# Hop fetches of edges without a successor: a bounds check and a cleared landing buffer, or a row of zeros in the table

## The reference

```python
A = 0.9 * segment_softmax(scores, head_ids)            # (edges, 4)
Z = broadcast(Z0[:, None, :], (nodes, 4, 64))
for _ in range(5):
    Z = segment_sum(A[:, :, None] * Z[tail_ids], head_ids) + 0.1 * Z0[:, None, :]
out = Z.reshape(nodes, 4 * 64) @ W_o
```

## Time and profile before

| | us |
|---|---|
| median of 3 runs | 11939.54 |
| lowest, highest | 11934.17, 11954.9 |
| span of the profiled execution, first to last instruction | 11926.9 |
| median over that span | 12.6 |
| window 2378 to 2916, hop 1 | 538 |
| window 4010 to 5046, hop 4 | 1036 |

### The profile page before, as it was taken

One profiled execution on the slowest core, in us unless ns is written; L12 is line 12 of the kernel. 1 busy time (PEld: TensorE's weight loads), 2 busy tenths in 40 slices (PEclk: granted clock), 3 DMA queues, 4 the chain that ended last, 5 costly groups with the idle time before them and its releaser, 6 DMA issues. The chain is left out here.

```text
span 11926.9 us, 102357 instructions
## 1 busy us (share of the span) xinstructions
PE 5189.3 (44%) x22423; PEld 3589.6 (30%) x22423; DVE 6264.4 (53%) x12751; ACT 2458.7 (21%) x4317; POOL 7982.4 (67%) x7869
## 2 busy tenths in 40 slices
PE   1719994000000244445655778833335422222245
PEld 1403221000000244444444556622224322222234
DVE  8931114887878544465555669933336533321127
ACT  0102221022222211122322333310003211000035
POOL 0767776776767677754766766567767677777730
PEclk9959997555555555576776777755555555555578
DMA  2412222554545211176654656622229833311148
GB/s 107 163 22 57 57 57 55 192 161 149 164 150 165 89 41 41 38 249 198 166 158 155 197 177 194 191 67 57 57 59 323 236 65 65 63 48 46 45 157 248
DMA packets 1247797, 1471.21 MB, mean 123 GB/s; under 512 B 843713, under 2 KB 948738, under 8 KB 1244410
## 3 DMA queue, kind: packets, MB, share of 16 engines
q1 hardware_dynamic: 951992, 1127.40, 29.9%
q0 software_dynamic: 277328, 269.94, 10.7%
q10 hardware_dynamic: 18290, 72.03, 1.5%
HBM read 830.95 MB, written 772.36 MB: 134 GB/s over the span
## 5 line engine op out<-in xcount | busy, mean ns | idle before, releaser
L2550 POOL DMA_INDIRECT r_got<-state,comb_src x1176 | 1209.8, 1029 | 454.9 <-issue 350.4
L330 POOL DMA_INDIRECT payload_or_bias_rows<-payload,place x784 | 885.2, 1129 | 587.4 <-POOLq L522 259.7
L1339 POOL DMA_INDIRECT hop_got<-edges_b,next_col x784 | 788.7, 1006 | 272.0 <-issue 238.5
L1339 POOL DMA_INDIRECT hop_got<-edges_a,next_col x784 | 782.1, 998 | 269.1 <-issue 238.4
L1588 PE MATMUL hop_ps_into<-hop_out,span_s 128*128 128x256 f32 (+1 forms) x10 | 5.6, 662 | 1966.6 <-DVE hop_out L1480 1965.8
L1528 ACT COPY hop_got<-hop_zeros 128x1792 f32<-128x1792 f32 x224 | 377.4, 1685 | 1508.7 <-DVE hop_ps_msg L1431 1099.0
L1588 PEld LDWEIGHTS hop_ps_into<-hop_out,span_s 128*128 128x128 f32 x10 | 2.5, 311 | 1969.1 <-DVE hop_out L1480 1968.1
L1480 DVE SCALAR_TENSOR_TENSOR hop_out<-hop_out,hop_runs_now,hop_ps_msg 128x256 f32<-128x256 f32 x1176 | 565.4, 481 | 51.0
L1351 POOL DMA_INDIRECT sum<-hop_out,put_s x392 | 432.3, 1103 | 119.5 <-issue 119.5
L2687 DVE TENSOR_REDUCE r_stat<-r_sq 128x14 f32<-128x896 f32 x196 | 211.9, 1081 | 567.8 <-ACT r_sq L2857 567.4
L2558 POOL DMA_INDIRECT x<-r_yt,put_t x392 | 403.8, 1030 | 146.6 <-issue 118.8
(11 more groups left out here) (727 smaller groups left out, 16895.6 us busy)
## 6 DMA issues: line engine op xcount, KB each, us to landing
edges_a<-hop_out SPq DMA_DIRECT2D x112, 896.0 KB
edges_b<-hop_out SPq DMA_DIRECT2D x112, 896.0 KB
hop_side<-x_dst SPq DMA_DIRECT2D x280, 224.0 KB, 4.0
r_in<-state SPq DMA_DIRECT2D x112, 448.0 KB, 4.9
x_and_sums<-c_y SPq DMA_DIRECT2D x56, 896.0 KB, 6.1
bn_in<-x_and_sums SPq DMA_DIRECT2D x56, 896.0 KB, 4.8
r_own<-state SPq DMA_DIRECT2D x84, 448.0 KB, 5.3
g_rows<-r_gx SPq DMA_DIRECT2D x84, 448.0 KB, 3.0
```

The costliest lines, as they stand in the source:

```text
L330: nc.gpsimd.indirect_dma_start(out=rows[:, n, :], out_offset=None, in_=t.pay, in_offset=bass.IndirectOffsetOnAxis(t.place[:, k, n:n + 1], ...
L1339: pool.indirect_dma_start(out=got[:, u, c, :], out_offset=None, in_=table, in_offset=at, bounds_check=EP - 1, oob_is_err=False).then_inc(g ...
L2550: pool.indirect_dma_start(out=got[:, n, c - b * CT, :], out_offset=None, in_=table, in_offset=bass.IndirectOffsetOnAxis(idx[:, at + c:at + ...
```

## The change

Hops no longer check the index, and the landing buffer is no longer cleared. An edge without a successor reads row EP of the table. The fetches of a chunk wait, in place of ACT's copy, for DVE's add of the chunk that used the same place before, four chunks earlier; `wait` issues nothing where the value is 0 or less, so the first four chunks wait for nothing. The semaphores `zeroed`, the tile `zeros`, DVE's fill and all of ACT's clearing copies go. Nothing else changes.

```diff
-        if heads and table is not None:
-            zeros = sb("zeros", [P, CT, G])
...
-        runs_ready, side_scaled, zeroed = sems("runs_ready"), sems("side_scaled"), sems("zeroed")
+        runs_ready, side_scaled = sems("runs_ready"), sems("side_scaled")
...
                 if heads:
-                    pool.wait_ge(zeroed[u], i + 1)
+                    wait(pool, added, n + 1 - RING)
...
                 for c in range(CT):
                     at = bass.IndirectOffsetOnAxis(idx[:, n * CT + c:n * CT + c + 1], 0)
-                    if heads:
-
-                        pool.indirect_dma_start(out=got[:, u, c, :], out_offset=None, in_=table, in_offset=at,
-                                                bounds_check=EP - 1, oob_is_err=False).then_inc(gathered[u], 16)
-                    else:
-                        pool.indirect_dma_start(out=got[:, u, c, :], out_offset=None, in_=table, in_offset=at
-                                                ).then_inc(gathered[u], 16)
+                    pool.indirect_dma_start(out=got[:, u, c, :], out_offset=None, in_=table, in_offset=at
+                                            ).then_inc(gathered[u], 16)
...
-            if heads and table is not None:
-                nc.vector.memset(zeros[:], 0.0)
             nc.vector.memset(acc[:, 1, CT - 1, 0:M], 0.0).then_inc(blank, 1)
...
-            if heads and table is not None:
-                act.wait_ge(blank, 1)
-                for u in range(RING):
-                    nc.scalar.copy(got[:, u], zeros[:]).then_inc(zeroed[u], 1)
-
...
-                    if heads and table is not None:
-                        act.wait_ge(added, order(i, u) + 1)
-                        nc.scalar.copy(got[:, u], zeros[:]).then_inc(zeroed[u], 1)
```

## The result

The changed kernel takes 12045.97 us (median of 4 runs, 12035.71 to 12086.14) against 11941.57 us for the kernel before. The ratio is 1.0091, with an interval of 1.0074 to 1.0107: slower by 0.9%, where 0.8% faster was forecast. The profiled execution has a span of 12033.9 us, 107.0 more than before.

A forecast was written before the change was run, and what follows sets the result against it. POOL's descriptor making was taken to bound all four fetching hops; 63.5 + 21.2 + 18 - 2 = 101 us off the 11926.9 us span gives 11826, plus 12.6 to the median makes 11839 us; range 11826 to 12074.

The forecast's parts named there:

- As that is under 1.249, it costs only a later landing: Hops' fetches: repeated zero-row reads, shorter than POOL's 1.249 us a fetch, only delay each hop's end, 0.5 us x 4 = 2 us.
- 0.84 us a fetch: Time for 77 reads of the zero row in one fetch, at 11 ns each, taken from the 256 B Chebyshev fetch.
- Rival B: Hops 1 to 3: the two queues' times add, 9.3 us a chunk; about 11935 us, no change; chance 0.10.
- The broadcast row's bound of 18 ns: A broadcast reading one 3.5 KB row 100 times allows at most 18 ns a repeated read, 1.39 us a fetch.
- Rival A: Hops 1 to 3: HBM's serving of row EP chokes the fetches (over 1.336 us each); slower, 12074 us or more; chance 0.26.
- ACT's wait past 4 us: Sign of being wrong: ACT's side-load wait exceeds its 4.0 us of cover at the new pace and the add waits for ACT.
- The bytes: Fetches grow from 52.5 to 131 KB; queue 0 takes 36% of the engines, queue 1 40%, together 76%, which fits.
- The check: Unchecked fetches in hops 1 to 4 take 944 ns in place of 998, gaining 63.5 us and 21.2 us.
- The starts: Without the clearing, each of four hops starts about 4.5 us earlier, 18 us in all.
- ACT's copies: The 224 clearing copies in the loops are hidden by POOL's pace, so removing them is worth nothing.
- The new wait: Fetches waiting for the add four chunks earlier have over 20 us of slack, so it costs nothing.
- Rival C: The check is free or not really removed; only 16 us stay, 11924 us, within the noise; chance 0.05.

The follow-up runs named there:

- e11_short_store: The changed kernel with the stores of hops 1 to 3 cut to 128 KB a chunk, every hop fetching from the first table: 11870.75 us, one run.
- e9_all_one: The changed kernel with all 128 rows of every fetch in hops 1 to 4 read from row EP: 12750.31 us, one run.
- e10_all_one_short: The changed kernel with all 128 rows of a fetch from one row and stores of hops 1 to 3 cut to 128 KB: 12548.4 us, one run.
- e5_spread: The changed kernel with edges without a successor reading 128 different rows of zeros in place of one: 11854.09 us, ratio 0.9913 to the kernel before.
- e7_two_rows: The changed kernel with two rows of zeros in place of one, odd partitions reading row EP + 1: 11836.55 us, ratio 0.9902 to the kernel before.
- e12_two_checked: The changed kernel with two rows of zeros and the bounds check put back, bound EP + 1: 11920.86 us, ratio 0.9978 to the kernel before.
- e6_checked_hot: The kernel before with the check's bound raised by one so row EP is read; check, clearing and old wait kept: 12096.98 us, ratio 1.0139.
- e8_side4: The changed kernel with four side buffers in place of two: 12106.78 us, ratio 1.0121 to the kernel before.

## Why the prediction was wrong

**The step that failed** is "As that is under 1.249, it costs only a later landing", for which the sum had 2 us. It set 0.84 us a fetch against POOL's pace, as if nothing else needed the sixteen engines, and so it put at nothing what the reads do to the side load. e11_short_store keeps POOL's 8.75 us a chunk with these very reads beside short stores. Beside the full stores, in the kernel after, a chunk takes 10.0 us: 141 us lost and 12.5 won at three starts are 154 us, or 0.92 us in each of the 168 chunks.

**What stood in its place** is told by two readings. First, the engines. In the kernel after, queue 0 holds the sixteen for 0.640 x 480 / 349 = 0.88 us a fetch, or 6.2 us for seven, and both queues together hold them for 92.7% of the time. Before, in the same 2400 to 2880, it was 52.1%:

```profile
q1 hardware_dynamic: 15184, 60.22, 38.1%
q0 software_dynamic: 17713, 19.32, 14.0%
```

Two rows of zeros take queue 0 to 0.370 x 460 / 369 = 0.46 us a fetch. Queue 1's own transfers are not slower: they hold the engines for 0.381 x 480 / 60.22 = 3.0 us a MB before and for 0.287 x 480 / 54.06 = 2.5 after. Hence I read the late side load as one that waits its turn behind the reads of the row, which is argued and not shown. Rival B had such a sum ("7 x 0.84 + 3.4 = 9.3 us a chunk"); I gave it 0.10, and it was too mild. But the engines are not full, so adding up their time doesn't by itself give the 10.0 us.

Second, the loop that the late side load closes. SP issues the load of chunk n + 1 behind the store of chunk n - 1, some 0.9 us after DVE's last link of it. Then come L us until ACT uses the rows, 0.74 us of ACT and 7.87 us of DVE's own work: for two chunks 9.5 + L. At POOL's 8.75 us a chunk there is room for an L of 8 us. Where every add waits for its side rows, the sum holds: e9_all_one has an L of 18.1 us, which makes 13.8 us a chunk for 14.1 measured over hop 1, and e10_all_one_short 15.4 us, which makes 12.4 for 12.7. In the kernel after, past the first eight chunks, L swings between 4.0 and 18.6 us; the 33 late loads of 56 cost time, and the early ones give none back.

**The size.** The 0.84 us is close to the 0.88 measured, but by chance. It is the stretch over which the engines worked on one fetch in quiet, and in the 1.4 us around it they were busy for 23.0%, which is 0.32 us of all sixteen:

```profile
q0 software_dynamic: 32, 0.03, 23.0%
```

Rivals A and B used the same 0.84 as time that the engines are held. The broadcast row's bound of 18 ns held (15.9 and at most 14.5 ns a read with all 128 reads on one row), and the pieces of a row are served side by side for the most part: 14.5 ns at most for 1 KB, not 44. The Trainium skill, DMA: Bandwidth & Descriptors, section How a descriptor splits into AXI transactions, gives four transactions for such a row; beside the 11 ns of 256 B, the 14.5 ns agree with their overlapping almost wholly.

**Rival A** named the right place and sign, and the measured time lies in its part of the range. Its price fits: at 10.0 / 7 = 1.43 us a fetch, 1176 x (1.43 - 1.303) - 39 = +110 us, measured +104. Its mechanism, fetches that are themselves too slow for POOL's pace, is not what was seen: DVE waited for fetched rows three times in 500 us of hop 1, and for the side rows 29 times.

**The side load.** I wrote that it has 4.0 us of cover for whatever the busier queues add, and did not price it. They added 4.7 us at the mean, from 4.8 to 9.5, and up to 14. I had named ACT's wait past 4 us as a sign of being wrong; it was 428.8 / 48 = 8.9 us, and the add waited for ACT 29 times. Only the two together tell: with two rows of zeros ACT, freed of its copies, waits 5.3 us a chunk for the side rows too (281.2 us in 53 waits), and no add waits for it.

**The bytes** were forecast well, 131 KB a fetch, and by e5_spread and e7_two_rows 35 to 37% of the engines: 36 was written. So the bytes are not the cause. Queue 1 stayed at 34 to 36%, where 40 was written.

**The gains.** The check: 54 ns forecast, 52 seen, so 63.5 + 21.2 = 85 us, and 84 by e12_two_checked. But in the kernel after only hop 4's part of it was won. Where the loop of the side load sets the pace, a shorter fetch gives POOL time to wait and nothing more: a chunk of hop 1 takes 10.0 us there and 10.1 in e6_checked_hot, with the check. The starts: 4.15 us each in place of 4.5. ACT's copies: nothing beyond the starts, as forecast, though no run removed them alone. The new wait: nothing while DVE keeps up (e7_two_rows); in the kernel after it passes DVE's lateness to POOL but is no cause (e6_checked_hot). Rival C fell.

With two rows of zeros the kernel lands at 11836.55 us, and 11839 was forecast for the change as it stood. That they meet so closely is luck in part. The two medians are of different chips; against the kernel before on its own chip the gain is 112 us, not 101, and 14 us of it are the scatters of hop 4, which nobody touched. The ratios put that version 0.98% ahead of the kernel before and 1.9% ahead of the kernel after. The 12.6 us that I added to the span are no fixed distance either: the profiled execution of the kernel after lasted 12035.71 us, 1.8 us over its span.

## What to carry to other kernels

A default row that many gathers share is a hot spot: spread it over a few copies, two were enough here. When a transfer gets slower, add its time on the DMA engines to that of everything else that they must move in the same period, instead of holding it against the issuing engine's pace alone. And look first at the load with the shortest lead: the 224 KB of side rows, issued one chunk ahead, not the fetches, issued up to four chunks ahead, were what everyone waited for. Last, when a buffer is made deeper, see in the trace that the load really starts earlier: in e8_side4 it did not.

## What I had not expected of the hardware

The effect has a knee. From one row to two, queue 0 falls from 64.0 to 37.0% of the engines; from two to 128, no further (35.4%). Its hold on the engines also depends on what else runs: with 77 repeated reads it is 0.88 us a fetch beside full stores and 0.519 x 400 / 320 = 0.65 beside short ones. With all 128 reads on one row it is 1.6 us either way. Why, no run shows.

The scatters of hop 4 became shorter, from 1103 ns on average to 1081, and to 1089 in e5_spread and 1067 in e7_two_rows, though nothing of them was changed; no run was made to explain it.

One chip ran the kernel before in 14480 us where others took 11942 to 11951, and hid a change worth 1% either way.
